# Text layers as one unrolled pipeline of 64 quads, image convolutions as a deeper pipeline with later loads

## The reference

```
# image: x is (64, 128, 64, 3)
h = layernorm(x.reshape(b, t, 192));  h = relu(conv2d(h, conv1_w (128,128,5,3)))
h = layernorm(h.reshape(b, t, 192));  h = relu(conv2d(h, conv2_w (128,128,5,2)))
h = layernorm(h.reshape(b, t, 128));  h = relu(conv2d(h, conv3_w (256,128,5,2)))
res = layernorm(h as (b, t, 128)) @ out_w + out_b
# text: 64 x 77 tokens, D = 64, 8 heads of 8, FF = 256, 4 layers
x = emb[tokens] + positions
for i in range(4):
    q = x @ Wq[i] + bq[i];  k = v = x @ Wv[i] + bv[i]
    o = softmax(q k^T / sqrt(8)) v          # per sample and head
    x = x + layer_norm(o @ Wo[i] + bo[i], ln1)
    y = gelu(x @ W1[i] + b1[i]) @ W2[i] + b2[i]
    x = x + layer_norm(y, ln2)
x = layer_norm(x, fin)
```

## Time and profile before

| what | us |
|---|---|
| median of 3 runs (lowest, highest) | 2695.6 (2692.45, 2728.44) |
| profiled execution, its span | 2723.24, 2721.4 |
| PE busy, DVE busy, ACT busy, POOL busy | 2250.7, 1816.3, 1344.1, 1207.3 |
| convolutions | from 29.6 to 526.9 |
| text layers | from 575.7 to 1750.2 |
| fusion attention and experts | to 2721.4 |

### The profile page before, as it was taken

How to read it: one execution, slowest core, us unless ns; L and a number is a source line. 1 busy time by engine, 2 the same in 40 slices (tenths; PEclk the granted TensorE clock), 3 DMA queues, 4 the chain that set the end, 5 groups by cost and what they waited for, 6 DMA issues and landing times. The chain is left out here.

```text
span 2721.4 us, 62098 instructions
## 1 busy us (share of the span) xinstructions
PE 2250.7 (83%) x19897; PEld 1805.2 (66%) x19897; DVE 1816.3 (67%) x5614; ACT 1344.1 (49%) x3116; POOL 1207.3 (44%) x1523
## 2 busy tenths in 40 slices
PE   5699999768886888778977888448888899699998
PEld 5699999656665766666765666436666676466665
DVE  3355565367755677467755775568888865588888
ACT  2122222125544555545554554557666655566663
POOL 2233333225546555655554554654444432443442
PEclk8899999869988999889887998759999955699999
DMA  5100000000000000000000000000000000000000
GB/s 124 29 12 17 12 17 6 1 1 1 0 1 1 1 0 0 0 2 0 0 1 1 1 0 1 0 1 0 0 0 0 0 0 1 4 10 9 8 9 11
DMA packets 39551, 19.18 MB, mean 7 GB/s; under 512 B 29508, under 2 KB 38852, under 8 KB 39366
## 3 DMA queue, kind: packets, MB, share of 16 engines
q1 hardware_dynamic: 39466, 18.00, 2.7%
HBM read 14.63 MB, written 3.36 MB: 7 GB/s over the span
## 5 line engine op out<-in xcount | busy, mean ns | idle before, releaser
L456 PE MATMUL im_c<-im_a_hi,im_w 128*128 128x256 f32 (+2 forms) x1920 | 429.4, 318 | 46.8 <-POOL im_a_lo L353 46.8
L456 PEld LDWEIGHTS im_c<-im_a_hi,im_w 128*128 128x128 f32 x1920 | 321.4, 191 | 63.3 <-POOL im_a_lo L353 47.6
L1064 POOL TENSOR_TENSOR tx_KB<-tx_KF,tx_head_rows 128x1248 fp32r<-128x1248 f32 x128 | 288.0, 2270 | 48.7 <-DVE tx_KF L932 48.7
L456 PE MATMUL im_c<-im_a_lo,im_w 128*128 128x256 f32 (+2 forms) x960 | 304.1, 317 | 0.0
L874 POOL TENSOR_TENSOR tx_rstd<-tx_var_eps,tx_power 77x4 f32<-77x4 f32 x128 | 130.7, 1021 | 369.6 <-DVE tx_var_eps L870 369.0
L1135 ACT ACTIVATE tx_PT<-tx_scores_t 77x624 f32<-77x624 f32 x256 | 175.3, 685 | 163.5 <-PE tx_scores_t L1278 154.1
L1278 PE MATMUL tx_scores_t<-tx_QP,tx_KB 128*77 128x78 f32 x2048 | 201.4, 250 | 9.9 <-DVE tx_QP L952 4.2
L946 DVE TENSOR_REDUCE tx_mpad<-tx_scores 77x8 fp32r<-77x616 f32 x256 | 202.3, 790 | 6.5 <-PE tx_scores L1260 5.9
L346 POOL TENSOR_TENSOR im_rstd<-im_var_eps,im_power 128x4 f32<-128x4 f32 x64 | 68.6, 1073 | 305.0 <-DVE im_var_eps L274 305.0
L1278 PEld LDWEIGHTS tx_scores_t<-tx_QP,tx_KB 128*77 128x77 f32 x2048 | 183.1, 157 | 29.5 <-DVE tx_QP L952 29.4
L456 PEld LDWEIGHTS im_c<-im_a_lo,im_w 128*128 128x128 f32 x960 | 182.7, 190 | 8.4
(11 more groups left out here) (312 smaller groups left out, 5977.7 us busy)
## 6 DMA issues: line engine op xcount, KB each, us to landing
im_x<-x SPq DMA_DIRECT2D x16, 384.0 KB, 3.3
out<-h_img SPq DMA_DIRECT2D x32, 64.0 KB
tx_toks<-x_txt SPq DMA_DIRECT2D x1, 1925.0 KB
im_raw<-L_tok_conv_w SPq DMA_DIRECT2D x1, 1280.0 KB, 8.9
out<-h_txt SPq DMA_DIRECT2D x32, 38.5 KB
im_raw<-L_tok_conv_w SPq DMA_DIRECT2D x1, 960.0 KB, 4.7
im_raw<-L_tok_conv_w SPq DMA_DIRECT2D x1, 640.0 KB, 6.1
tx_raw_W<-L_txt_W SPq DMA_DIRECT2D x2, 256.0 KB, 5.8
```

What stands on the lines that cost most here:

```text
L456: last = pe.matmul(acc[:, :, d0:d1], w[c][:, slot, part], img[:, b0_:b1_, d0 + shift:d1 + shift, kj:kj + J], start=opens, stop=closes)
L1064: pool.tensor_tensor(KB[:, par, t], KF[:, t].bitcast(F32).unsqueeze(1).broadcast_to([P, HPT, QW]), head_rows[:].unsqueeze(2).broadcast_to( ...
```

## The change

In the image branch `a_hi` and `a_lo` of all three convolutions get two buffers. In step n PE runs the first convolution of quad n, with the transposes and the projection of quad n-3 after its two halves, then the second of quad n-1 and the third of quad n-2. The x load runs two quads ahead, and the later stages' loads are issued in step U-2. Semaphores are kept per convolution, and DVE signals only its last instruction of a group.

In the text branch the two loops and the phases go. One step per n, from -2 to N+5 with N = 64 (layer times quad), is written out without loops on every engine. Step n holds the attention of quad n with the projections of n+1, the attention's norm of n-1, its sum of n-2 (`sum_a`, formerly `mid_sum`), the transpose for the feed-forward of n-3, `down` of n-5 with its norm, and its sum of n-6 (`sum_y`, four instructions like `sum_a`, in place of `ln_apply` and `end_sum`). `up` runs in even steps only, for n-5 and n-4, and writes the banks `work[0]` and `work[1]`, which transposes, projections, `project_o` and `down` use as well. The weights are read from `w_all`, `w2_all`, `rows_all`, `cols_all` in place; the copies and the fifth, empty layer of these tiles go. The two norms have tiles of their own, and `xs_f` joins `xs`. `first_on_work0(n)` and `first_on_work1(n)` wait until the last readers of the two banks are done (`qk_cut`, `oT_set`, `fT_set`; `v_set`, `a_scaled`, `y_scaled`; and `f_gelu` of the second quad in even steps). The end of the stage, the final norm, only has its semaphores renamed. The core of the diff, image branch first (SP, DVE, PE), then text (DVE, POOL, ACT, PE):

```diff
-a_hi = [sb(f"im_a_hi{c}", [P, (2 if c == 0 else 1), QUAD, COLS[c], JP], F32R) for c in range(3)]
+a_hi = [sb(f"im_a_hi{c}", [P, 2, QUAD, COLS[c], JP], F32R) for c in range(3)]
...
+def each_quad(eng, step):
+    for n in range(-1, 4):
+        step(n, n % 2)
+    with eng.Fori(2, U // 2 - 1) as i:
+        step(i * 2, 0)
+        step(i * 2 + 1, 1)
+    for n in range(U - 2, U + 3):
+        step(n, n % 2)
...
-        def step(n, par, first, last):
-            if not last:
-                if not first:
-                    sp.wait_ge(normed_ready, (n * 3 - 2) * QUAD)
-                load(n + 1, 1 - par)
-            if first:
+        def step(n, par):
+            if here(n + 2):
+                if past(n + 1):
+                    sp.wait_ge(normed_ready[0], n * QUAD + QUAD)
+                load(n + 2, par)
+            if isinstance(n, int) and n == U - 2:
                 for inputs in later_loads:
                     inputs.load(sp)
-        each_quad(sp, lambda: load(0, 0), step)
+        load(0, 0)
+        each_quad(sp, step)
...
+        def step(n, par):
+            k, full = Count(norms_before(n, ALL)), Count(norms_before(n, FULL))
+            third_cut = (lo_ready[2], n - 1) if past(n - 1) else None
+            if here(n + 1):
+                dve.wait_ge(x_loaded[1 - par], (n + par) * 8 + 16)
+                normalise(xin[:, 1 - par], 0, 3 * J, g0, b0, k, full, third_cut)
+            if here(n - 3):
+                last_norm(n - 3, k)
+            if here(n):
+                normalise(act_out[0], 1, 3 * J, g0, b0, k, full,
+                          (lo_ready[0], n + 2) if here(n + 1) else third_cut,
+                          half_ready=(relu_done[0], n * 2 + 1))
+            if here(n - 3):
+                store_rows(n - 3)
+            if here(n - 1):
+                dve.wait_ge(relu_done[1], n)
+                normalise(act_out[1], 2, 2 * J, g1, b1, k, full,
+                          (lo_ready[1], n + 1) if here(n) else third_cut)
...
-        def step(n, par, first, last):
-            cuts = cuts_before(n)
-            two_before = not isinstance(n, int) or n > 1
-            conv(0, par, 1 if first else n * 3 - 1, n, (lambda: project(n - 2)) if two_before else None)
-            if not first:
-                conv(2, 0, cuts, n - 1)
-            conv(1, 0, cuts + (1 if last else 2), n)
-            if not first:
-                turn_res(n - 1)
-            if last:
-                project(n - 1)
-                conv(2, 0, cuts + 2, n)
-                turn_res(n)
-                project(n)
-        each_quad(pe, lambda: None, step)
+        def step(n, par):
+            if here(n):
+                first_conv(n, par, 0)
+            if here(n - 3):
+                turn_res(n - 3)
+            if here(n):
+                first_conv(n, par, 1)
+            if here(n - 3):
+                project(n - 3)
+            if here(n - 1):
+                second_conv(n - 1, 1 - par)
+            if here(n - 2):
+                third_conv(n - 2, par)
+        each_quad(pe, step)
...
+xs_f = sb("xs_f", [P, QUAD, 2 * D], F32R)
...
+rows_of_work1 = work[1][0:R, 0:QUAD * D].rearrange("p (b d) -> p b d", b=QUAD)
...
+N = LAYERS * U
+A_NORM, F_TURN, F_DOWN, F_SUM = 1, 3, 5, 6
...
+        def step(n):
+            now, ahead, before = live(n), live(n + 1), live(n - 1)
+            if before:
+                normalise_o(n - 1, 3)
+            if now:
+                find_max(n, 2)
+            if ahead:
+                cut_qk(n + 1, 0)
+                cut_qk(n + 1, 1)
+            if now:
+                join_max(n, 2)
+                normalise_o(n, 0)
+                find_max(n, 3)
+            if ahead:
+                cut_qk(n + 1, 2)
+                cut_qk(n + 1, 3)
+            if live(n - F_SUM):
+                sum_y(n - F_SUM)
+            if now:
+                join_max(n, 3)
+                normalise_o(n, 1)
+            if ahead:
+                set_v(n + 1)
+            if live(n - 2):
+                sum_a(n - 2)
+            if ahead:
+                find_max(n + 1, 0)
+            if now:
+                normalise_o(n, 2)
+            if ahead:
+                join_max(n + 1, 0)
+                find_max(n + 1, 1)
+            if live(n - F_DOWN):
+                scale_y(n - F_DOWN)
+            if ahead:
+                join_max(n + 1, 1)
+            if live(n - F_DOWN):
+                var_y(n - F_DOWN)
+            if before:
+                scale_a(n - A_NORM)
+                var_a(n - A_NORM)
...
+        def step(n):
+            if live(n - F_TURN):
+                cut(quads(n - F_TURN), xs_f, f_hi, f_cut, n - F_TURN)
+            if live(n - 1):
+                cut(o_rows[:, (n - 1) % 2], os_, o_hi, o_cut, n - 1)
+            if live(n + 1):
+                split_k(n + 1)
+            if live(n - 1):
+                shift(n - 1, a_shift, None, "ln1_b", a_shifted)
+            if live(n + 2):
+                cut(quads(n + 2), xs, x_hi, x_cut, n + 2)
+            if live(n - F_DOWN):
+                shift(n - F_DOWN, y_shift, x_mid, "ln2_b", y_shifted)
+                power_of(n - F_DOWN, y_var_eps, y_rstd, y_var, y_power)
+            if live(n - 1):
+                power_of(n - 1, a_var_eps, a_rstd, a_var, a_power)
...
+                act.wait_ge(f_up, q * 2 + half + 1)
+                act.activation(HT[:, q % 2, half], work[half][:, 0:QW], ACT.Gelu, bias=col(q, 8 + half))\
+                    .then_inc(f_gelu, 1)
+        def step(n):
+            if live(n):
+                exp(n, 0)
+            if live(n - 1):
+                copy_outs(n - 1, 3)
+            if n % 2 == 0 and live(n - 5):
+                gelu(n - 5)
+            if n % 2 == 0 and live(n - 4):
+                gelu(n - 4)
+            if live(n + 1):
+                set_turned(n + 1, xT, x_turned, xT_set)
+                part_lo(n + 1, 0)
+                part_lo(n + 1, 1)
+            if live(n - 1):
+                act.wait_ge(o_set, n * QUAD)
+                hi(n - 1, o_rows[:, (n - 1) % 2], os_, o_hi)
+            if live(n - F_TURN):
+                act.wait_ge(x_mid, n - F_TURN + 1)
+                hi(n - F_TURN, quads(n - F_TURN), xs_f, f_hi)
+            if live(n):
+                exp(n, 1)
+                copy_outs(n, 0)
+            if live(n + 1):
+                part_lo(n + 1, 2)
+                part_lo(n + 1, 3)
+            if live(n):
+                exp(n, 2)
+                copy_outs(n, 1)
+            if live(n + 2):
+                if n + 2 >= U:
+                    act.wait_ge(x_new, n + 2 - U + 1)
+                hi(n + 2, quads(n + 2), xs, x_hi)
+            if live(n - 1):
+                set_turned(n - 1, oT, o_turned, oT_set)
+            if live(n - F_DOWN):
+                square(n - F_DOWN, y_square, y_made, y_squared)
+            if live(n):
+                exp(n, 3)
+                copy_outs(n, 2)
+            if live(n - F_TURN):
+                set_turned(n - F_TURN, xTf[:, (n - F_TURN) % 2], f_turned, fT_set)
+            if live(n - 1):
+                square(n - A_NORM, a_square, a_made, a_squared)
...
+        def step(n):
+            now, ahead, before = live(n), live(n + 1), live(n - 1)
+            even = n % 2 == 0
+            if now:
+                score_t(n, 0)
+            if before:
+                weigh(n - 1, 3)
+            if now:
+                turn_max(n, 1)
+                score(n, 2)
+            if even and (live(n - 5) or live(n - 4)):
+                pe.wait_ge(fT_set, min(n - 3, N))
+                if live(n - 2):
+                    pe.wait_ge(a_scaled, n - 1)
+                elif live(n - 6):
+                    pe.wait_ge(y_scaled, n - 5)
+            if even and live(n - 5):
+                up(n - 5)
+            if before:
+                turn_outs(n - 1, 3)
+            if even and now:
+                score_t(n, 1)
+                weigh(n, 0)
+            if even and live(n - 4):
+                if live(n - 5):
+                    pe.wait_ge(f_gelu, (n - 5) * 2 + 2)
+                up(n - 4)
+            if ahead:
+                first_on_work0(n)
+                turn(xs, n + 1, x_cut, x_turned)
+                pe.wait_ge(xT_set, n + 2)
+                project(n + 1, 0)
+                first_on_work1(n)
+                project(n + 1, 1)
+            if now:
+                if not even:
+                    score_t(n, 1)
+                    weigh(n, 0)
+                turn_max(n, 2)
+                score(n, 3)
+            if ahead:
+                project(n + 1, 2)
+                project(n + 1, 3)
+            if now:
+                turn_outs(n, 0)
+                score_t(n, 2)
+                weigh(n, 1)
+                turn_max(n, 3)
+            if ahead:
+                project_v(n + 1)
+            if now:
+                turn_outs(n, 1)
+            if before:
+                if ahead:
+                    pe.wait_ge(qk_cut, n * 4 + 7)
```

(55 more changed lines are left out.)

949 lines of the change are left out of this document (319 added, 630 removed).

## The result

The changed kernel takes 3149.79 us (median of 4 runs, 3130.72 to 3172.36) against 2712.02 (4 runs, 2692.45 to 2737.22): ratio 1.1645, interval 1.1487 to 1.1804. The forecast was 2741 with a range to 2860; it is 290 us past that end. The profiled execution's span is 3128.9 us, 407.5 above the 2721.4 of before.

| stage | before | after | difference | forecast |
|---|---|---|---|---|
| up to the text layers | 575.7 | 555.4 | -20.3 | -34 |
| text layers | 1174.5 | 1634.6 | +460.1 | +79.5 |
| behind them | 971.2 | 938.9 | -32.3 | 0 |

The account below looks back on a forecast made before the run. TensorE was taken to pace the convolutions, no single engine the attention. Image -33, removed copies -1 and text +79.5 gave +45.5 on the profiled 2723.2 (2769), or 2741 against the 2695.6 median; range 2550 to 2860.

Parts of the forecast that it names:

- Image, forecast -34: Image stage: three inner stalls go (-32.9), start and restarts -5, added step wait +5, so -33; removed memsets and copies -1.
- The added step time: Image steps: third-norm transposes wait for DVE's last norm, 0.4 us a step, 13 steps, +5 us.
- 14.0 less 13.75: Image step: DVE needs 14.0 us for its norms; PE's transposes come 13.75 us after the second convolution ended.
- The walk's main wait: Text step, traced along the engine queues: DVE's last join waits 2.1 us for a max PE turns after project_o, behind scale_y.
- The walk's 16.9 for an odd step: Text: odd step by DVE's account, work 12.3 us plus idle waits, sum 16.9; even step 22.0.
- the sums at 1.41 us: Text step on DVE: the second sum of four instructions priced at 1.41 us from the old sum's row.
- costs nothing: Text step on POOL: 10.1 us of work; its K split ends at 11.4, needed at 12.5, so no cost.
- A: The forecast itself: text steps of mean 19.4 us a quad, text +79.5, total 2741, own range 2690 to 2800; chance 0.45.
- rival C: Text: PE's clock falls to half, a step about 26 us; a quarter of steps +98, 2839, all over 3100; chance 0.17.
- Table loads, forecast 1.28 once a pair: Text on ACT: about 64 table loads, one pair per even step, with 1.28 us exposed once.
- Rival D: Text: a table switch also empties ACT, another 1.28 us or so on each of 64, up to +82, some 2800; chance 0.06.
- Rival B: Text: old quads' work fills idle time, step 16.1 us, text -119, total 2542; decides below 17.9; chance 0.30.

Follow-up runs that it names:

- e8: Image part alone on the kernel before, last three image steps reordered so convolutions precede quad n-3's transposes and projection: 2699.9 us, ratio 0.9948.
- e11: Changed kernel with both sums and both scales moved on DVE, plus ACT's exp and output copy ahead of the two hi copies in even steps: 2732.3 us, 1.0148.
- e7: Changed kernel with sum_y moved behind sum_a, and scale_y and scale_a moved earlier on DVE: 2782.5 us, ratio to before 1.0286.
- e10: Changed kernel with scale_y and scale_a early, sum_y behind find_max(n, 2) and sum_a behind scale_y: 2796.8 us, ratio to before 1.0358.
- e5: Changed kernel with sum_y behind sum_a, plus dummy transposes filling PE's waits ahead of project_o and up: 2930.4 us, ratio to before 1.0811.
- e6: Changed kernel with sum_y behind sum_a and scale_y moved ahead of normalise_o(n, 2) on DVE: 2822.2 us, ratio to before 1.0389.
- e3: Changed kernel with gelu replaced by identity with bias, so no table loads: 3158.0 us, ratio to before 1.1619.
- e9: Changed kernel with sum_y late, scale_y and scale_a early, and gelu replaced by identity so no table loads: 2711.8 us, ratio to before 1.0065.

## Why the prediction was wrong

**Image, forecast -34, measured -20.** The three stalls inside went. The added step time was 0.2 us, not 0.4; the working's own terms, 14.0 less 13.75, give 0.25. The first convolution starts 1.0 us later (30.61, 29.61 before). What failed is the account of the end: the working had 16 equal steps and none for the drain, where PE takes the transposes of quad n-3 ahead of a convolution that is ready (4.98 + 0.87 + 4.73 + 0.87 us, at half clock behind them). e8 gives 6.6 of it back.

**The walk's main wait was right.** It said that the last join would wait 2.1 us behind `project_o` and `scale_y`; the trace after has 2.18 on DVE, and 1.39 on PE. It said even steps would be 5.1 us longer than odd ones; they are 6.1, in part by luck, since odd steps hold the longer `sum_y` and even ones more half clock. At full clock, in e11, the difference is 5.25. The walk's 16.9 for an odd step stands beside e7's 16.15 at full clock, which no longer has the `scale_y` wait but has 1.23 us behind `sum_a`, and beside e10's 15.06, which has neither. The trace of the changed kernel has 61 table loads in the text (64 forecast), and SP's later loads come after all image loads.

**The step that failed: the sums at 1.41 us.** `sum_y` was priced by the row of the old sum, 1.48 us for four instructions. That row stands beside two of POOL's small instructions (POOL in the kernel before):

```profile
665.54 0.73 POOL L882 TENSOR_TENSOR tx_x_shift<-h_txt,tx_rows 77x256 f32<-77x256 f32 x1
666.24 0.72 POOL L1057 TENSOR_TENSOR tx_xs<-h_txt,tx_xs 77x256 fp32r<-77x256 f32 x1
```

Where POOL is idle the four take 0.86, so the price already held some of this wait, but of instructions of 0.7 us. The diff put `sum_y` behind the cuts of Q, beside POOL's copies of K of 2.27 us each, which the walk itself had ending at 11.4 us of an odd step, while it had `sum_y` done at 10.2. The prediction says "costs nothing" of POOL because its queue had room; what POOL does to DVE beside it was not asked. Measured: 4.79 and 3.09, that is 5.1 us a pair above the price, of the 12.2 us by which the pair shown exceeds the walk. The sign was there: in the kernel before, single instructions of this sum take up to 0.86 us, with a median of 0.27.

**The second: full clock in the forecast.** A was summed at 1.00; rival C, with a chance of 0.17, priced the clock apart, at a quarter of the steps. The profile has 0.70, that is 60% of the time at half clock. C is not an alternative to A: it came on top of A's waits and of the 3.5 us that A did not have. In the pair shown, each of the two falls follows a wait, of 3.50 and of 1.22 us, though not each such wait brings a fall (e5). C's "over 3100" for all steps and its 26 us for a step at half clock are near the measured 3150 and 25.6 by luck: the measured mean holds 40% of its time at full clock and 3.9 us of `sum_y`, and PE waits in every step. What the clock costs: 65 us with two waits filled (e5), and of the 162 of e6 the 88 beyond the wait itself, as far as that sum can be split.

**Table loads, forecast 1.28 once a pair.** In the changed kernel they cost nothing that can be told (e3), since another wait stood there; in e7 2.6 us a pair, the clock's share in it included (e9). Rival D, that a switch also empties ACT, is not borne out by the timeline of e7: the load starts 0.02 us after ACT's last instruction ends and gelu starts 0.01 us after the load. The drain of 1.38 us that the Trainium skill adds ("ScalarE: Activation LUTs", section "What ACT_TABLE_LOAD costs") is not seen beside the loads of e7 or of the changed kernel.

**Rival B**, that the overlap pays, fell: its step of 16.1 us is reached by odd steps alone, and not before two groups of instructions were moved (e6). Its decision point was a mean step of 17.9; e11's 17.7 at full clock would just pass it, but the clock's mean there is 0.91, the mean step 18.4, and the text takes 1223.5.

What stays open: of e11's 49 us above the loops of before, how much is the clock and how much the shared banks (a version with the feed-forward matmuls in banks of their own was not tried); what pattern of waits makes the clock fall; and what the clock added to the changed kernel as a whole, since no run holds it at 1.00.

## What to carry to other kernels

Before moving a VectorE instruction with two SBUF inputs, lay its new place over GpSimd's timeline, not only over its own queue: the price of an instruction is a price beside certain neighbours. Where each step of a tight pipeline holds TensorE waits like the 1.2 to 3.5 us of this one, price the step at both clock levels: removing such a wait gave about twice its length in e6, and filling it with dummy work gave part of that in e5. And when an experiment that removes a cost shows nothing, repeat it after the next wait is gone.

## What the runs showed of the hardware

Four VectorE instructions with both inputs in SBUF, 0.27 us each, took 4.79 us beside GpSimd. The first did not pass at the boundary between two GpSimd copies (1019.6) but at the end of the second, the others each at the end of a GpSimd instruction. VectorE instructions with one input in PSUM kept their length beside the same copies. Adding 14 transposes a step (10, and 8 in even steps) made a kernel 65 us faster in its stage. The stage behind the text, with the same code in all kernels, took between 938.9 us (changed kernel) and 985.4 (e10) in the profiles; in the kernel before PE stood at half clock there while busy 19.5 of 20 us, so a level of the clock is not explained by idle time alone. Differences under some 45 us of the whole kernel are safer read from the stage that was edited, where the scatter of the untouched text loops was 14 us.
